# Macaron block on one core: the routing steps of phases 2 to 13 in slots of their own, and the next x's halves turned before the weights

## The reference, cut to what matters

```
x = x + 0.5 * ffn(layernorm(x))
x = x + attn(layernorm(x))
x = x + 0.5 * ffn(layernorm(x))

ffn(x):  shared = silu(x @ Ws_up) @ Ws_down
         aff    = x @ centroids.T                        # 64 experts
         idx    = top_k(aff + expert_biases, 8)
         w      = sigmoid(aff[idx]);  w = w / (sum(w) + 1e-8)
         cw     = zeros(T, 64).at[idx].add(w)            # weight of each expert, by row
         routed = sum_e cw[:, e] * (silu(x @ W_up[e]) @ W_down[e])
         return shared + routed
```

## Time and profile before

| what | value |
|---|---|
| median of 3 runs | 788.37 us |
| the profiled execution | 788.31 us |
| its span, first to last instruction | 786.5 us |
| busy share PE / DVE / ACT / POOL | 97% / 80% / 81% / 68% |
| granted TensorE clock | 0.998 of full speed |
| DMA engines busy, transfers | 11.2% |

### The profile page before, as it was taken

The page is one execution under the profiler, slowest core; times in us unless marked ns, Lnnn a source line. Parts: engine busy times, 40 slices in busy tenths (PEclk is TensorE's granted clock), DMA queues, the critical chain, the costliest instruction groups (busy, mean ns, idle before and its releaser), DMA issues.

```text
span 786.5 us, 11865 instructions
## 1 busy us (share of the span) xinstructions
PE 766.5 (97%) x3425; PEld 619.5 (79%) x3425; DVE 629.3 (80%) x1376; ACT 634.8 (81%) x1225; POOL 534.8 (68%) x559
## 2 busy tenths in 40 slices
PE   8999999999999999999999999999999999999998
PEld 6777877887868878788786887778877787888786
DVE  6787989888687796978969788686887778787875
ACT  7987778788887888869888698786888778786885
POOL 4785646676857767677776787676877767664453
PEclk9999999999999999999999999999999999999999
DMA  8000000011101111001110012010120110000000
GB/s 287 15 1 14 15 1 8 14 41 48 28 7 28 47 40 33 13 14 47 40 33 13 13 47 53 20 26 21 26 53 20 27 27 24 25 0 1 14 2 13
DMA packets 63069, 23.57 MB, mean 30 GB/s; under 512 B 49344, under 2 KB 61888, under 8 KB 63040
## 3 DMA queue, kind: packets, MB, share of 16 engines
q1 hardware_dynamic: 63040, 23.21, 11.2%
HBM read 9.05 MB, written 2.10 MB: 14 GB/s over the span
## 4 chain that ended last, share of the span: by engine, by line
PE 61%; DVE 19%; ACT 12%; issue 6%; POOL 1%; DVEq 0%; ACTq 0%
PE up L1064 10%; PE y_ps L1064 10%; PE y_ps L1066 9%; PE y_ps L1065 9%; PE up L1066 9%; PE up L1065 9%; ACT up L652 5%; ACT g_hi L690 4%; DVE g_lo L917 4%; DVE gated L908 4%; DVE up L908 2%; DVE taken L872 2%; DVE w_sel L879 1%; ACT sh_low L619 1%; DVE biased L859 1%
## 5 line engine op out<-in xcount | busy, mean ns | idle before, releaser
L438 POOL TENSOR_TENSOR g_lo<-gated,g_hi 128x512 fp32r<-128x512 f32 x256 | 332.3, 1299 | 187.5 <-ACT g_hi L690 186.5
L652 ACT ACTIVATE up<-up 128x512 f32<-128x512 f32 x512 | 299.7, 586 | 68.3 <-PE up L1066 66.3
L908 DVE TENSOR_TENSOR gated<-up,cw 128x512 f32<-128x512 f32 x256 | 176.1, 688 | 89.1 <-ACT up L652 80.4
L1064 PE MATMUL up<-x_hi,wu_hi 128*128 128x512 f32 x512 | 204.0, 398 | 10.9 <-DVE g_lo L917 10.4
L908 DVE TENSOR_TENSOR up<-up,cw 128x512 f32<-128x512 f32 x256 | 177.1, 692 | 37.4 <-ACT up L652 35.5
L1064 PE MATMUL y_ps<-g_hi,wd_hi 128*128 128x512 f32 x512 | 202.6, 396 | 1.2 <-POOL g_lo L438 1.1
L1065 PE MATMUL up<-x_lo,wu_hi 128*128 128x512 f32 x512 | 200.2, 391 | 0.0
L1066 PE MATMUL up<-x_hi,wu_lo 128*128 128x512 f32 x512 | 200.0, 391 | 0.0
L1065 PE MATMUL y_ps<-g_lo,wd_hi 128*128 128x512 f32 x512 | 199.6, 390 | 0.0
L1066 PE MATMUL y_ps<-g_hi,wd_lo 128*128 128x512 f32 x512 | 199.5, 390 | 0.0
L690 ACT CAST g_hi<-up 128x512 fp32r<-128x512 f32 x256 | 150.9, 590 | 41.5 <-DVE up L908 40.3
(11 more groups left out here) (164 smaller groups left out, 552.9 us busy)
## 6 DMA issues: line engine op xcount, KB each, us to landing
x_in<-in_x SPq DMA_DIRECT2D x8, 256.0 KB, 2.8
wu_raw<-in_w_up SPq DMA_DIRECT2D x4, 512.0 KB, 7.1
wd_raw<-in_w_down SPq DMA_DIRECT2D x4, 512.0 KB, 7.8
x_res<-in_x SPq DMA_DIRECT2D x8, 256.0 KB, 2.7
out<-out_sb SPq DMA_DIRECT2D x7, 256.0 KB, 2.2
mix<-in_mix SPq DMA_DIRECT2D x1, 389.0 KB, 6.5
n_turned_halves<-n_halves SPq DMA_TRANSPOSE x17, 2.7
out<-out_sb SPq DMA_DIRECT2D x2, 128.0 KB, 1.9
```

The lines of the kernel that those rows point to most:

```text
L438: nc.gpsimd.tensor_tensor(g_lo[:, i, :], gated[:, t // 2 % ORING, :], g_hi[:, i, :].bitcast(fp32), ALU.subtract).then_inc(lo_done[1], 1)
L652: nc.scalar.activation(up[i][:, :], up[i][:, :], ACT.Silu).then_inc(silu_done, 1)
L908: nc.vector.tensor_tensor(gated[:, t // 2 % ORING, :] if t % 2 else up[i][:, :], up[i][:, :], cw[ph.q][:, :], ALU.mult).then_inc(gate_done, 1)
L1064: nc.tensor.matmul(o, a[0], b[0], start=start, stop=False)
```

## The change

It moves steps to other slots, in three tables, and swaps two DMA issues on SyncE. No instruction is added, removed or changed in size. In the order slot before -> slot after:

- phase 2: bias 11 -> 13, sig 12 -> 14, max 12 -> 14, take 12 -> 15, gate 12 -> 19, sum 12 -> 20, inv 15 -> 21, cw_pack (17, 21) -> (22, 24), cw_join (25, 27) -> (28, 30), stat1 (10, 12) -> (9, 10), aggr1 13 -> 12, rstd1 14 -> 13
- A phases: sh_low 14 -> 15, bias 14 -> 16, sig 15 -> 17, max 15 -> 18, take 15 -> 19, gate 16 -> 21, sum 16 -> 22, inv 18 -> 23, cw_pack (19, 21) -> (24, 25), stat0 (9, 10) -> (8, 9), aggr0 12 -> 10, rstd0 15 -> 11, shift0 18 -> 14, norm0_act (19, 21) -> (16, 18), x_pack (25, 27) -> (20, 22), keep 23 -> 19; cw_join and x_join stay
- B phases: sh_low 9 -> 11, sig 10 -> 14, bias 10 -> 14, max 11 -> 15, take 11 -> 16, gate 12 -> 18, sum 12 -> 19, inv 15 -> 20, cw_pack (18, 20) -> (21, 22), cw_join (27, 28) -> (28, 30); the mixing block's steps stay

```diff
 AT_STEADY_A = {
-    "y": 2, "x2_join": (3, 5), "x_split": 7, "y_join": (9, 11), "sum_out": 17, "keep": 23,
-    "aff": 11, "aff_pack": 11, "sh_silu": 12, "sh_high": 13, "sh_low": 14, "aff_join": 13,
-    "bias": 14, "sig": 15, "max": 15, "take": 15, "gate": 16, "sum": 16, "inv": 18, "cw_pack": (19, 21), "cw_join": (29, 31),
-    "stat0": (9, 10), "aggr0": 12, "rstd0": 15, "shift0": 18, "norm0_act": (19, 21), "x_pack": (25, 27), "x_join": (33, 34),
+    "y": 2, "x2_join": (3, 5), "x_split": 7, "y_join": (9, 11), "sum_out": 17, "keep": 19,
+    "aff": 11, "aff_pack": 11, "sh_silu": 12, "sh_high": 13, "sh_low": 15, "aff_join": 13,
+    "bias": 16, "sig": 17, "max": 18, "take": 19, "gate": 21, "sum": 22, "inv": 23, "cw_pack": (24, 25), "cw_join": (29, 31),
+    "stat0": (8, 9), "aggr0": 10, "rstd0": 11, "shift0": 14, "norm0_act": (16, 18), "x_pack": (20, 22), "x_join": (33, 34),
 }
 AT_STEADY_B = {
-    "x_split": 1, "aff": 4, "aff_pack": 4, "sh_silu": 5, "sh_high": 6, "sh_low": 9, "aff_join": 9,
-    "sig": 10, "bias": 10, "max": 11, "take": 11, "gate": 12, "sum": 12, "inv": 15, "cw_pack": (18, 20), "cw_join": (27, 28),
+    "x_split": 1, "aff": 4, "aff_pack": 4, "sh_silu": 5, "sh_high": 6, "sh_low": 11, "aff_join": 9,
+    "sig": 14, "bias": 14, "max": 15, "take": 16, "gate": 18, "sum": 19, "inv": 20, "cw_pack": (21, 22), "cw_join": (28, 30),
...
@@ -395,8 +395,8 @@
                 load_res(c)
+                turn_x(c + 1)
                 turn_weights(2 * c - 1)
-                turn_x(c + 1)
```

More of the change, by code:

```diff
@@ L92 @@
     "x_split": 3, "aff": 8, "aff_pack": 8, "sh_silu": 9, "sh_high": 10, "sh_low": 11, "aff_join": 11,
-    "sig": 12, "bias": 11, "max": 12, "take": 12, "gate": 12, "sum": 12, "inv": 15, "cw_pack": (17, 21), "cw_join": (25, 27),
-    "y_t": 6, "x1": 8, "stat1": (10, 12), "aggr1": 13, "rstd1": 14, "norm1": (16, 18), "xu": 19, "u_t": 22,
+    "bias": 13, "sig": 14, "max": 14, "take": 15, "gate": 19, "sum": 20, "inv": 21, "cw_pack": (22, 24), "cw_join": (28, 30),
+    "y_t": 6, "x1": 8, "stat1": (9, 10), "aggr1": 12, "rstd1": 13, "norm1": (16, 18), "xu": 19, "u_t": 22,
     "u_copy": 22, "attn": 25, "tanh": 25, "gamma": 25, "x2": (27, 28),
```

## The result

| | before | after |
|---|---|---|
| median us | 788.40 (4 runs, 788.28 to 788.91) | 776.24 (4 runs, 776.00 to 777.09) |
| profiled execution, its span | 788.31, 786.5 | 776.00, 773.7 |
| up(9) to up(25), phase 6 (B) | 24.40 | 23.32 |
| up(9) to up(25), phase 7 (A) | 23.52 | 22.50 |
| up(1) to up(9), phase 7 | 9.29 | 9.46 |

The ratio is 0.9846, with a 95% interval of 0.9829 to 0.9864: 12.2 us less, where 12.3 were forecast.

A forecast was written before the change was run, and what follows sets the result against it. TensorE sets the pace, waiting for the up product's bank freed by DVE's low_part. Gains of 6.0 (B) + 5.0 (A) + 0.8 (phase 13) + 0.5 (phase 2) = 12.3 us take 788.3 to 776 us; range 772 to 780, wider 768 to 783.

The forecast's parts named there:

- The criterion: Phases 3 to 12: PE stalls at up(t) once gate(t - 4) starts over about 4.1 us after up(t - 4).
- A phases: Slots 14 to 23: no stall left, 1.0 us gained of up to 1.08 a phase; five give 5.0 us.
- B phases: Stalls and restarts fall from 2.64 to 1.44 us; 1.2 us gained a phase, 6.0 us over five.
- The new stalls: B phases: lateness behind low(10), low(14), low(16), low(20) of 0.07, 0.07, 0.5, 0.36 us, plus 4 x 0.11 for restarts.
- The pile on ACT: B's slots 14 and 15: sig and two norm halves, 2.3 us in two slots, leave low(14) 0.07 us late.
- Operations held by POOL: DVE steps starting behind a POOL operation block; in B select takes about 0.9 us, w_norm up to 1.29.
- The weights' join: cw_join's data comes in time: 0.3 us to spare in A's slot 29; six slots from pack to join in B.
- cover: B: u's last piece ends at 336.8, TensorE needs it at 337.2; costs nothing, with 0.2 us of cover.
- already level: B, kernel before: u's last piece ended at 338.47 and the mixing products began at 338.73, read as level.
- the sum: Whole kernel: 6.0 (B) + 5.0 (A) + 0.8 (phase 13) + 0.5 (phase 2) = 12.3 us, 1.6%.
- POOL waits for w_norm: Sign named in advance, at cw_pack in B's slot 21: if seen, the prediction is wrong.
- rival 4: B's u chain: late w_norm holds POOL at cw_pack, delaying u_join, g_lo(21), mixing products; slower, 793 us at 3.5 us; chance 0.11.

The follow-up runs named there:

- a_only: The kernel before with only the A phases' table and SyncE's swapped order from after; 782.76 us, ratio 0.9926.
- a_odd: The kernel after with the A phases' shift0 in slot 13 instead of 14 and bias in 15 instead of 16; 776.17 us, ratio 0.9848.
- b_sig_10: The kernel after with the B phases' sig back in slot 10 from 14; 772.72 us, ratio 0.9798.
- b_odd: The kernel after with the B phases' bias, gate, sum and inv one slot earlier (13, 17, 18, 19); 774.36 us, ratio 0.9818.
- b_join_27: The kernel after with the B phases' cw_join back in slots 27 and 28 from 28 and 30; 775.42 us, ratio 0.9834.
- best: After with B's bias 13, gate 17, sum 18, inv 19, sig 10, sh_low 12, cw_pack (22, 24), cw_join (27, 28), phase 2's cw_join (27, 28); 768.76 us.

## Why the prediction was right, point by point

**The bound and its size.** The criterion (gate(t - 4) over 4.1 us behind up(t - 4)) holds: in after gate(9) trails by 3.75 and up(13) starts on time; gate(21) trails by 4.85 and up(25) is 0.43 us late against up(24). It holds at every late start of phase 6: with gate(t - 4) trailing by 4.32, 4.25, 4.55, 4.72 and 4.85 us, up(t) starts 5.66, 5.60, 5.90, 6.05 and 6.18 us after up(t - 4), each 1.33 to 1.35 us more than the lag.

**A phases.** 1.0 forecast a phase, 1.04 measured over five; a_only shows that it is A's alone. The count behind it was too kind: it had gate(15) to gate(23) trail by 1.7 to 2.8 us, and they trail by 3.13 to 3.90. The shift started 0.02 us after POOL's g_lo(13) and took 1.29 us. The forecast says that its lags hold even with bias, shift and w_norm held, but its 1.7 us for gate(15) has no room for a held shift: a_odd, where the shift takes 0.15, has 1.93. w_norm was not held at all (0.42). The whole fitted under 4.1 with 0.2 to spare, and a_odd shows that the missing time was free.

**B phases.** 1.2 us forecast; measured 0.47 + 0.61 = 1.08 up to up(25) and 0.17 behind it, 1.25 in all. The new stalls were forecast at up(15), 19, 21 and 25 with 0.07, 0.07, 0.5 and 0.36 us, 1.0 in all (each with 0.06 us between the end of low_part and the start on PE, which the text does not name). They came at up(15) with 0.22, up(19) with 0.02, up(21) with 0.30 and up(25) with 0.43, and at up(23), forecast in time, with 0.05: 1.02 in all. The sum is right and the places are right but for one; that the parts add up to 1.0 with such differences between them is in part luck. The restarts cost more than the 4 x 0.11 forecast: 0.12 to 0.14 us in each of the slots 15, 19, 21 and 23, 0.54 up to up(25). At up(15) the step at fault is low_ahead in 11, which I let cost 0.60; from its start to gate(11) it is 0.71, as in the earlier trace rows (317.31, and gate(9) behind it at 318.02). The pile on ACT was named rightly, and b_sig_10 shows that it alone carried 0.74 us a phase, more than my count of its lateness (0.07 at two places) would give.

**Operations held by POOL.** In B select was forecast as held, at 0.9, and w_norm as held, at up to 1.29: they took 1.20 and 1.04. That bias would be held too, at 1.36, was not in the count of B; it cost nothing, as b_odd's gate(15) shows. The rule of the Trainium skill (SBUF — State Buffer, "Who interferes with whom" and its summary for kernel authors), that the one that starts second blocks fully, fits the rows on bias, select and shift. The trace differs a little in the size: bias and select end 0.29 us behind POOL and not the 0.41 that they take alone.

**The queues.** The weights' join had its data in time, as counted. u's last piece ended at 332.42 + 0.18 = 332.60 and the mixing products began at 332.96, 0.36 us later; where they wait for it, they begin 0.26 to 0.28 later, so about 0.1 us of cover was left, where 0.2 was forecast. The forecast read the kernel before wrongly here: it calls u's last piece and the mixing products "already level", but they stood 0.40 us behind the last matmul where 0.23 is the distance without a wait, so they waited 0.17 us a phase. That wait went with the change and with it the mixing products' own restart, while up(25) now holds a restart of 0.10: 0.17 us net, which the sum does not hold.

By its own words the prediction was also to be wrong if POOL waits for w_norm, and POOL does, 0.45 us ahead of cw_pack in each of the five B phases. This was a bad sign to choose, since the count itself had POOL waiting there, and the wait did not reach TensorE.

In b_odd the mixing products wait again, 0.20 us beyond the undisturbed distance, but not in the way of rival 4: w_norm was there at 329.10, long before POOL came to the pack at 330.90. It is POOL's own order that holds u's last piece.

**What the sum missed.** cw_join moved from 27 and 28 to 28 and 30 in B, and to 28 and 30 in phase 2. I had checked only that its data would be there, not what stands behind it on POOL (rstd2 and g_lo(31)). It cost 0.155 x 6 = 0.9 us, shown by b_join_27 and best. Phase 2 gave 0.8 instead of 0.5 and B's end 0.8 more, which covered it. So 12.3 against 12.1 is closer than the parts deserve: that the forecast met the time to 0.2 us is luck, while the stalls it named and their size in A and B are not.

## What to carry to other kernels

Where three engines chase a fourth through a ring of banks, work out how far the chain may trail before the ring runs dry, and place side work so that the lag stays below it; below it nothing more is gained, above it each 0.1 us is paid, and a start that comes late by only 0.02 us already pays the restart of 0.12 us or more. Look at the piles on every engine of the chain: here moving one 0.8 us step on ACT (0.74 us a phase) was worth more than moving four on DVE by one slot (0.57). And when a step moves on an in-order queue, look at what stands behind its new place too, and not only at whether its input is there.

## What the runs showed of the hardware

A DVE operation on two SBUF operands that starts behind one of POOL's operations on two tiles of 128x512 ends just after it, however small it is: those of 128x256 elements 0.27 to 0.29 us behind POOL's end, the shift of 128x4 elements 0.01 to 0.03 us (366.85 + 1.29 against 366.83 + 1.29), which made 1.29 us of 0.15. Where the DVE operation starts first, it takes its usual time and POOL's is the longer one. w_norm in phase 7 of the kernel after is such a case, 0.08 us ahead of POOL's g_lo(23), which takes 1.49 us instead of 1.29:

```profile
381.69 0.42 DVE L899 SCALAR_TENSOR_TENSOR w_norm<-w_sel,w_inv 128x256 f32<-128x256 f32 x1
381.77 1.49 POOL L438 TENSOR_TENSOR g_lo<-gated,g_hi 128x512 fp32r<-128x512 f32 x1 [0.44 <-ACT g_hi L690]
```

And a restart of PE behind a wait costs more than the wait: the first matmul shows 0.50 us instead of 0.39, the next one starts 0.33 or 0.34 us behind it instead of 0.23, and the slot is 0.12 to 0.14 us longer, even where the wait was 0.02 us.
